# Projection, norms and routing of batches 0 to 2 moved in between the attention steps

## The reference, cut to what matters

```
x = layernorm(x + attention(x))            # 16 heads of 64, softmax over 1024 keys, then Wp and bp
m = concat(x[:, ...], compression, ctx)    # per batch: rows shifted, 4:1 convolution of 154 old rows
x = layernorm(x-like rows m + x)           # the "memory" block: moved rows, conv rows, context rows
x = layernorm(x + moe(x))                  # top-1 router, 8 experts, capacity 1024/8 per batch
```

## Time and profile before

| | us |
|---|---|
| median of three runs | 2067.19 |
| profiled execution | 2064.02 |
| its span | 2062.3 |
| first pair to last `o_out` (end) | to 1598.54 |
| first expert matmul | 1841.09 |
| PE busy in the span | 1923.6 (93%) |
| DVE, ACT, POOL busy | 1312.0, 871.3, 1353.8 |

### The profile page before, as it was taken

How to read it: one execution, slowest core, us unless ns; L and a number is a source line. 1 busy time by engine, 2 the same in 40 slices (tenths; PEclk the granted TensorE clock), 3 DMA queues, 4 the chain that set the end, 5 groups by cost and what they waited for, 6 DMA issues and landing times. The chain is left out here.

```text
span 2062.3 us, 30831 instructions
## 1 busy us (share of the span) xinstructions
PE 1923.6 (93%) x11352; PEld 1269.5 (62%) x11352; DVE 1312.0 (64%) x2294; ACT 871.3 (42%) x1103; POOL 1353.8 (66%) x710
## 2 busy tenths in 40 slices
PE   7999999999999999999999999999998767659996
PEld 5665665566556655566566556655653767648886
DVE  5566666666666666666666666666663556657775
ACT  3444444444444444444444444444443344314553
POOL 2677777777777777777777777777777213435554
PEclk8999999999999999999999999999999888759998
DMA  3000000000000001000000000000011754223331
GB/s 107 12 21 16 22 16 27 16 21 16 22 16 22 16 26 26 17 22 16 22 16 22 21 22 16 22 16 22 16 26 42 232 148 134 67 92 105 126 131 42
DMA packets 145807, 92.71 MB, mean 45 GB/s; under 512 B 73852, under 2 KB 133372, under 8 KB 145660
## 3 DMA queue, kind: packets, MB, share of 16 engines
q1 hardware_dynamic: 142588, 82.28, 14.1%
q0 software_dynamic: 3072, 8.46, 1.1%
HBM read 61.81 MB, written 25.23 MB: 42 GB/s over the span
## 5 line engine op out<-in xcount | busy, mean ns | idle before, releaser
L309 POOL TENSOR_TENSOR prob_sum<-prob_sum,probs 128x1024 f32<-128x1024 f32 x384 | 913.4, 2379 | 200.9 <-ACT probs L481 159.2
L530 DVE TENSOR_REDUCE max_of<-spare_ps 128x1 f32<-128x512 f32 x1024 | 656.6, 683 | 437.0 <-PE spare_ps L382 435.9
L481 ACT ACTIVATE probs<-score_ps 128x1024 f32<-128x1024 f32 x512 | 515.7, 1027 | 535.1 <-PE score_ps L403 531.2
L417 PE MATMUL av_ps<-probs,v 128*64 128x512 f32 x2048 | 467.6, 599 | 0.5 <-DVE o_out L548 0.5
L417 PEld LDWEIGHTS av_ps<-probs,v 128*64 128x64 f32 x2048 | 138.9, 137 | 269.7 <-issue 248.8
L382 PE MATMUL spare_ps<-k_hi,q_hi 64*128 64x512 f32 x1024 | 292.6, 558 | 10.1 <-DVE max_of L530 6.5
L382 PEld LDWEIGHTS spare_ps<-k_hi,q_hi 64*128 64x128 f32 x1024 | 166.7, 306 | 209.6 <-issue 204.1
L305 POOL TENSOR_TENSOR prob_sum<-probs 128x1024 f32<-128x1024 f32 x64 | 153.5, 2399 | 188.2 <-ACT probs L481 188.2
L542 DVE RECIPROCAL recip<-sums 128x128 f32<-128x128 f32 x256 | 232.7, 931 | 36.1 <-ACT sums L493 35.8
L403 PE MATMUL score_ps<-q_hi,k_hi 64*128 64x512 f32 x1024 | 213.4, 397 | 1.6 <-DVE xT_rest L554 0.9
L403 PE MATMUL score_ps<-shift_rows,one_rows 64*128 64x512 f32 x1024 | 211.0, 393 | 0.0
(11 more groups left out here) (189 smaller groups left out, 2509.8 us busy)
## 6 DMA issues: line engine op xcount, KB each, us to landing
o_transposed<-o_out SPq DMA_DIRECT2D x64, 256.0 KB, 2.0
xT_kept<-o_transposed SPq DMA_DIRECT2D x32, 512.0 KB, 4.7
w_raw<-in_L_ffn_W_dram SPq DMA_DIRECT2D x16, 1024.0 KB, 5.9
w_raw<-in_L_attn_Wq_dram SPq DMA_DIRECT2D x64, 64.0 KB, 2.3
w_raw<-in_L_attn_Wk_dram SPq DMA_DIRECT2D x64, 64.0 KB, 2.2
wv_raw<-in_L_attn_Wv_dram SPq DMA_DIRECT2D x32, 128.0 KB, 2.7
x<-in_x_dram SPq DMA_DIRECT2D x4, 1024.0 KB, 7.1
xe<-expert_rows SPq DMA_DIRECT2D x7, 520.0 KB, 4.0
```

The costliest lines, as they stand in the source:

```text
L309: pool.tensor_tensor(out, out, probs[:, n % RING], ALU.add).then_inc(prob_added, 1)
L417: last = pe.matmul(av_ps[hd * E:(hd + 1) * E, :], v[:, quad % 2, kt, 2 * first_head + hd, :], probs[:, n % RING, hd, :], start=(kt == 0), ...
L481: act.activation(probs[:, n % RING], score_ps[n % 2][:, :, :], ACT.Exp).then_inc(probs_ready, 1)
L530: dve.tensor_reduce(max_of[:, u % 2, kh, j, hd:hd + 1], bank[:, :], AX.X, ALU.max).then_inc(pass_read, 1)
```

## The change

`build_project_route` is gone. A class `Route` holds its buffers, semaphores and every step as a method with the engine as an argument. Inside `build_attention`, `steps_of` yields route steps behind the first bite of each half: `route.plan(b - 1, s)` for half s (0 to 31) of batch b, so batch b - 1's projection, norms and routing run during the attention of batch b. One tile is projected in each of the halves 3 to 10; the first norm is in 11 to 13, the moves in 14, the sums in 15 and 16, compression in 16, the second norm in 17 to 19, transposes and logits in 19 to 23, `choose` in 24, the mask in 25, the tally in 26, counts in 27, `find_free` in 28, `find_rows` in 29, the sends in 30 and 31. The PE groups of these steps use the same three `spare_ps` banks. Batch 3 has a block of its own behind attention, `build_last_batch`, with eight banks and all its O tiles loaded at once, and not one step of another batch beside it. `EARLY_BATCHES` is 3.

To make room in SBUF: x^T is kept for two batches; that of batches 2 and 3 is computed at the start, stored to DRAM (`x_transposed`) and loaded into the place of batch 0 and 1 at halves 36 and 68; `w_raw` has one place instead of two; the ring `probs` has 8 places instead of 12; the reciprocal is written over `sums`; `x1` and `x2` hold one batch.

```diff
-EARLY_BATCHES = 2
+EARLY_BATCHES = 3
@@ class Route
+    def plan(self, b, s):
+        found = []
+        if s == 1:
+            found += [("load_x", b), ("load_o", 8 * b), ("load_o", 8 * b + 1)]
+        if 2 <= s <= 3:
+            found += [("bias", b, s - 2)]
+        if 3 <= s <= 10:
+            found += [("proj", 8 * b + s - 3)]
+            found += [("load_o", 8 * b + s - 1)] if s <= 8 else []
+        if 2 <= s <= 9:
+            found += [("split", 8 * b + s - 2)]
+        found += {11: [("aggr", 0, b), ("load_cw", b), ("ids", b), ("load_new", b)],
+                  12: [("scale", 0, b), ("norm1", b, 1)],
+                  13: [("norm1", b, 0), ("old", b)],
+                  14: [("move", b)],
+                  15: [("moved", b, 0)],
+                  16: [("moved", b, 1), ("comp", b), ("stats2", b, 0)],
+                  17: [("stats2", b, 1), ("aggr", 1, b)],
+                  18: [("scale", 1, b), ("norm2", b, 0)],
+                  19: [("norm2", b, 1)],
+                  24: [("choose", b)],
+                  25: [("mask", b)],
+                  26: [("tally", b)],
+                  27: [("count", b)],
+                  28: [("rows", b, 0)],
+                  29: [("rows", b, 1)],
+                  30: [("send", b, 0)],
+                  31: [("send", b, 1)]}.get(s, [])
+        if 20 <= s <= 23:
+            found += [("logits", b, s - 20)]
+        if 19 <= s <= 22:
+            found += [("x2T", b, s - 19)]
+        return found
...
+    def find_scale(self, dve, i, b):
+        dve.wait_ge(self.root_done[i], b + 1)
+        wait(dve, (self.x1_done, self.x2_done)[i], self.TB * b)
+        self.step(dve, dve.reciprocal(self.scale[i][:, :], self.root[i][:, :]))
+        dve.scalar_tensor_tensor(out=self.shift[i][:, :], in0=self.moments[i][:, :, 0], scalar=-1.0,
+                                 in1=self.scale[i][:, :], op0=ALU.mult, op1=ALU.mult).then_inc(self.shift_done[i], 1)
...
@@ build_attention
-    RING = 12
+    RING = 8
+    def route_steps(h):
+        b, s = divmod(h, HALVES // B)
+        if b > 0:
+            return route.plan(b - 1, s)
+        return {6: [("wp", 0)], 7: [("wp", 1)], 8: [("consts",)]}.get(s, [])
...
-            if name == "bite" and h < HALVES and START_OF[h] + i < END_OF[h]:
-                yield "bite", START_OF[h] + i
+            if name == "bite":
+                if h < HALVES and START_OF[h] + i < END_OF[h]:
+                    yield "bite", START_OF[h] + i
+                if i == 0 and h < HALVES:
+                    yield from route_steps(h)
...
-        if step[0] in ("bite", "sum"):
+        if step[0] in ("bite", "sum", "proj", "old", "comp", "x2T", "logits", "count"):
...
-        w_raw = sb("w_raw", [P, 2, 2, KC, P])
+        w_raw = sb("w_raw", [P, 2, KC, P])
-        xT = [xT_kept[:, b] for b in range(2)] + [xT_rest[:, b] for b in range(B - 2)]
+        xT = [xT_kept[:, b % 2] for b in range(B)]
...
 (POOL, at the end of each half, behind its adds)
+                for name, *at in route_steps(h):
+                    if name == "bias":
+                        route.bias(pool, *at)
+                    if name == "moved":
+                        b, i = at
+                        for t in route.SUM_ORDER[2 * i:2 * i + 2]:
+                            route.add_moved(pool, b, t, route.sum_done)
+                    if name == "send":
+                        route.send(pool, *at, route.sent)
...
+def build_last_batch(nc, route, weights):
+    (tensor)
+            for t in range(TB):
+                route.project(pe, T0 + t, y_bank[t])
+            pe.wait_ge(route.z_done, T0 + TB)
+            route.transpose_old(pe, b, old_bank)
+            route.compress(pe, b, comp_bank)
+            for g in range(TB // 2):
+                route.transpose_x2(pe, b, g, x2T_bank[g])
+            pe.wait_ge(route.comp_added, b + 1)
+            for g in range(TB // 2):
+                route.score_experts(pe, b, g, logits_bank[g])
+            route.count(pe, b, count_bank)
```

More of the change, by code:

```diff
@@ L503, in _ @@
                     total_out(*at)
-            early.split_wp_high(act)
+                if name == "wp":
+                    route.wp_high(act, *at)
+                if name == "split":
+                    route.split_high(act, *at)
+                if name == "aggr":
+                    route.take_root(act, *at)
+                if name == "norm1":
+                    b, i = at
+                    route.norm1(act, b, range(4 * i, 4 * i + 4))
+                if name == "norm2":
+                    b, i = at
+                    route.norm2(act, b, range(4 * i, 4 * i + 4))
+                if name == "x2T":
+                    route.x2T_out(act, *at, *spare((name, *at)))
+                if name == "choose":
+                    route.exp_gates(act, *at)
         @block.vector
@@ L567, in _ @@
                     normalise(*at)
+                if name == "split":
+                    route.split_low(dve, *at)
+                if name == "proj":
+                    route.add_projected(dve, *at, *spare((name, *at)))
+                if name == "aggr":
+                    route.aggregate(dve, *at)
+                if name == "scale":
+                    route.find_scale(dve, *at)
+                if name == "old":
+                    route.place_old(dve, *at, *spare((name, *at)))
+                if name == "comp":
+                    route.add_compressed(dve, *at, *spare((name, *at)))
+                if name == "stats2":
+                    b, i = at
+                    route.rows_stats(dve, b, range(4 * i, 4 * i + 4), route.sum_done, route.PLACES * b)
+                if name == "logits":
+                    route.read_logits(dve, *at, *spare((name, *at)))
+                if name == "choose":
+                    route.choose(dve, *at)
+                if name == "mask":
+                    route.find_mask(dve, *at)
+                if name == "tally":
+                    route.tally(dve, *at)
+                if name == "count":
+                    route.read_counts(dve, *at, *spare((name, *at)))
+                if name == "rows" and at[1] == 0:
+                    route.find_free(dve, at[0])
+                if name == "rows" and at[1] == 1:
+                    route.find_rows(dve, at[0])
 class ForProjection:
@@ new lines, in _ @@
+            for t in range(TB):
+                route.split_high(act, T0 + t)
+            route.take_root(act, 0, b)
+            route.norm1(act, b, range(HT, TB))
+            route.norm1(act, b, range(HT))
+            for j in range(weights.PIECES):
+                weights.split_high(act, 0, 0, j)
+            route.take_root(act, 1, b)
+            route.norm2(act, b, range(TB))
+            for g in range(TB // 2):
+                route.x2T_out(act, b, g, x2T_bank[g])
+            route.exp_gates(act, b)
@@ L1079, in _ @@
+            for j in range(weights.PIECES):
+                weights.split_high(act, 1, 0, j)
         @block.vector
         def _(dve):
[L1081 to L1094 removed]
@@ L1242, in build_experts @@
-def build_experts(nc, weights, x2, send_to, xe_dram, late_sent, out, const):
+            for t in range(TB):
+                route.split_low(dve, T0 + t)
+                if t > 0:
+                    route.add_projected(dve, T0 + t - 1, y_bank[t - 1])
+            route.add_projected(dve, T0 + TB - 1, y_bank[TB - 1])
+            route.aggregate(dve, 0, b)
+            route.find_scale(dve, 0, b)
+            route.place_old(dve, b, old_bank)
+            for t in (4, 6):
+                route.add_moved(dve, b, t, half_sum_done)
@@ L1246, in build_experts @@
+            route.find_free(dve, b)
+            route.find_rows(dve, b)
+def build_experts(nc, weights, route, xe_dram, late_sent, out, const):
     EX, D, HID = weights.W1.shape
@@ L1350, in send @@
                                             in_=y[:, e % 2, t, :], in_offset=None).then_inc(sent[e % 2], 16)
[L1352 to L1355 removed]
+            for i in range(2):
+                route.send(pool, B - 1, i, late_sent)
             for e in range(EX):
```

1122 lines of the change are left out of this document (575 added, 547 removed).

## The result

After: 2175.18 us (median of 4 runs, 2172.99 to 2179.02); before, beside it, 2066.64 (2066.01 to 2067.33, 4 runs). The ratio is 1.0527, 95% interval 1.0509 to 1.0545: slower by 5.3%, 108.5 us. The forecast was 2150, its range 2030 to 2190. The profiled execution has a span of 2171.7 us, 109.4 above the one before.

The account below looks back on a forecast made before the run. PE was taken to bound attention, idling 82 us behind it. Stage -150, experts -1, prologue +1, PE's work +107 and pauses +126 sum to +83 on 2062.3: span 2145, forecast 2150 us, range 2030 to 2190.

Parts of the forecast that it names:

- Stage, experts: Between last o_out and first expert matmul, 92.5 us for batch 3 alone in place of 242.5: -150; experts -1.
- the +6 for the port: Behind attention: low halves of expert weights on POOL stand against DVE's two-input operations, +6 us within the 92.5.
- PE's added work: In attention: 71 us for 24 projected tiles plus 36 for three batches' other route work, +107, bounds 103 and 115.
- Pauses: In attention: PE waits for other engines' queues 42 us a batch, +126 in all, bounds 39 and 237.
- The signs named beforehand: PE's attention waits at some 40 us a batch, longest at find_rows, mask, second root; small DVE operations reaching 2 us.
- The port: In attention: DVE's two-input operations wait for POOL's instructions; with own lengths 21.8 us a batch, bounds 3.2 and 40.
- rival (a): The port doesn't bite in attention: pauses 39 to 46, sum about 0 to +3, 2070 us; chance 0.2.
- the chains' sum: Late routing halves, per batch: choose 1.1, mask 5.0, tally 2, free rows 3, find_rows 10.7; in all 21.8 us.
- "zero" for the x^T reload: In attention: storing and reloading x^T of batches 2 and 3 (8 MB, DMA share 0.08) costs nothing.
- Sends: POOL's sends, four of 1.27 us behind each of two halves, cost 1.2 us a batch, bounds 0 and 5.
- paid in full: In attention all engines wait for PE, so whatever work is put on PE there adds its whole time.
- Rival (b): In attention queues refill during 3.5 us of value products, so only PE's added work counts: -43, 2024 us; chance 0.27.

Follow-up runs that it names:

- e9: Changed kernel with the same operations reordered: O tiles first, x^T reloads later, chains in VectorE's idle gaps, norms and sends moved; 2066.75 us, ratio 1.0019.
- e1: Changed kernel with GpSimd's 448 additions of the probabilities replaced by fills of about equal length that read nothing from SBUF; 2130.02 us, ratio 1.0295.
- e5: Changed kernel with O tiles 1 to 7 of batches 0 to 2 asked for at the head of SyncE's work; 2155.43 us, ratio 1.0432.
- e4: Changed kernel with only 4 of the 12 matmuls of each projection of batches 0 to 2; 2168.33 us, ratio 1.0490.
- e12: e9 with the first norm's statistics moved into VectorE's idle stretches, tally to the gap of half 25, count to half 26; 2086.06 us, ratio 1.0094.
- e6: e5 with also only 4 of the 12 matmuls of each projection of batches 0 to 2; 2148.15 us, ratio 1.0410.
- e2: Control: the kernel before with GpSimd's additions replaced by the same fills as in e1; 2071.47 us, ratio 1.0012.
- e11: Changed kernel with ACT.Exp in place of ACT.Sqrt in the roots of batches 0 to 2, so no table load there; 2169.94 us, ratio 1.0508.

## Why the prediction was right

**Stage, experts.** -150 forecast, -152.5 measured in that execution (90.0 us long against my 92.5; 89 to 96 in the profiled executions of the experiments, where this code is the same). Its parts fit as well: last norm done after 41.8 (42), moved pieces there 11.5 later (9.5), `send_to` 29.8 later (29.4), first expert 6.9 later (5.7); of the +6 for the port at most 3.4 show, the 90.0 less 86.6. Experts -1 against +1.3.

**PE's added work.** +107 forecast. It shows bare in e9: +111.6. In the changed kernel busy time rose by 147.5. The projection's matmuls are recorded with 80.7 us in three groups like the one below, where I had 71. That is no miss: the same 80.7 stand in e9 at clock 0.99, and the groups overlap; three starts of 0.96 a tile are 69 us for 24 tiles.

```profile
L380 PE MATMUL spare_ps<-wp_lo,o_hi 128*128 128x256 f32 x192 | 27.0, 283 | 0.0
```

**Pauses.** 126 forecast; 113 of idle and 36 of slow clock measured, 149. By place:

| three batches, us | forecast, with PE's work | measured |
|---|---|---|
| projection, s 3-11 | 71 + 25.5 = 96.5 | 109.7 |
| norms, old rows, logits, s 13-23 | 31.5 + 36 = 67.5 | 71.7 |
| chains, s 25-29 | 65.4 | 66.9 |
| sends, s 31 and 1 | 3.6 | 11.2 |

The signs named beforehand came as well: PE's idle time grew by 38 us a batch for "some 40", the longest pauses stand at find_rows (12.8) and the mask (8.0), both in the last batch, with the late O tile's 7.1 and 6.7, which I had not named, next to them, and small operations of VectorE took 2 us and more, at most 2.5; the 9.98 us of the earlier trace rows did not come back.

The port, weighed against rival (a), was the largest term, and e1 shows it at 48 us. In my sum it decided the sign, in the runs it did not: without the additions the kernel is still 61 us slower than before (1.0295), since other pauses stayed, where rival (a) had 2070. That the chains' sum fits to 2% is luck in good part. Of the 65.4 forecast some 10 were the operations' own lengths and 56 the port; e1 gives 45 to the additions and leaves 22. And I charged one GpSimd instruction for every two-input operation; in the timeline above several run in GpSimd's idle moments, so the unit at 29 (free rows and find_rows, 13.7 in my list) cost 7.8 and 7.6 in the first two batches. Against that the unit at 27 (tally, 2) cost 4.5 and 4.1, and the last batch cost 29.7 us in this column where the first two cost 18.9 and 18.3; its units at the end of the attention are shorter (17 us, nothing left to project), which I had not looked at.

**What I had wrong.** The "zero" for the x^T reload together with the late O tiles: 14 us in the projection's column, which without them (e5) stands at 96.1 for my 96.5. I had checked the reload's share of DMA time, not what is queued behind it. Missing altogether is the clock after a pause, 36 us of PE time: idle time alone (113) fell short of my 126, and the sum still came out higher. Windows of 12 us of the changed kernel, two with a pause and one without (PE's busy time is the first value after the length, the clock the third from the end):

```profile
698.00:710.00 12.00, 7.90 (x24) 3.02 (x26) 4.59 (x15) 5.83 (x6) 10.35 (x5) 0.57 0.06 23
866.00:878.00 12.00, 7.91 (x46) 6.16 (x48) 11.46 (x20) 3.67 (x4) 9.99 (x6) 0.79 0.01 0
470.00:482.00 12.00, 12.00 (x88) 8.87 (x84) 9.48 (x13) 4.57 (x6) 10.91 (x5) 1.00 0.02 2
```

Sends were 8 us under. The sum was 26 us low, +83 for +109. In the bounds, the low terms add up to 12 a batch and not 13 (36 for 39), and rival (a)'s pauses of 39 to 46 give a sum of -4 to +3, not 0 to +3. And that PE's work is "paid in full" holds for the unit taken apart above, but not in reverse: e4 took 46 us of it away and got 8 back, as other waits grew.

**Rival (b)**, that the queues refill and only PE's work counts, is no property of the change but of its order. e9 goes part of the way, to 2067: what follows the last `o_out` took 463.8 us before and 317.7 in e9, 146.1 less, and the attention took 145.8 more. Its 2024 was not reached, since the attention never grew by less than 145 with all of the work in it, where 107 were assumed: 112 of work and 34 of pauses.

## What to carry to other kernels

Work moved beside a full engine costs its own time plus what its queue position holds up; a step list has places where an engine is idle and its shared port too, and the same operations cost 1.6 us there and 7.9 us elsewhere. Before a bulk transfer is called hidden, look at what stands behind it in its queue and who stands still for that, not at the DMA's share. Where removing much of an engine's work returns almost nothing, compare the mean lengths of the other engines' instructions before and after: what was removed may have moved one of them to a worse place, as it did the subtraction, from 1.42 to 2.49 us.

## What the runs showed of the hardware

- A chain of eight 128x8 additions on VectorE, 1.57 us beside an idle GpSimd, took 7.93 beside four GpSimd additions that filled 9.89 us (e12). Operations of 64 elements and of 8 are held alike; the hold ends with GpSimd's instruction (871.98 and 871.89 us in the changed kernel).
- GpSimd's fills of the same length do not hold VectorE's operations with two SBUF inputs (the eight additions fell from 410 to 193 ns each on average, e1), but they did hold a one-input TENSOR_SCALAR of 8 elements for 0.83 us.
- A subtraction of 128x1024 on VectorE took 1.23 us where GpSimd only filled (e1) and 2.49 on average beside its additions (e6).
- Pauses of PE of 2 to 8 us, and one of 12.8, went with a clock of 0.96 and 36 us of slowed matmuls on top of 113 us of idle time; where no wait for `max_of` passed 2.3 us (e9) the clock was 0.99.
- The attention repeats within 0.07 us a unit in another run of the same steps (e2, but for its last two units), finer than any whole time here.
- A table load on ScalarE took 1.28 us; with 12 of them gone (15 us of ScalarE's time) some 6 us came back in the units concerned (e11).
